# First attention of a two-layer kernel: TensorE's second pair of score maxima set directly behind the scores

## The reference, cut to what matters

```python
def _L0_xattn_ref(x, y, wq, bq, wk, bk, wv, bv, wo, bo):   # 16 heads of 8
    q = (x @ wq + bq).reshape(B, Sq, H, D).transpose(0, 2, 1, 3)
    k = (y @ wk + bk).reshape(B, -1, H, D).transpose(0, 2, 1, 3)
    v = (y @ wv + bv).reshape(B, -1, H, D).transpose(0, 2, 1, 3)
    scores = jnp.einsum('bhqd,bhkd->bhqk', q, k) / jnp.sqrt(jnp.asarray(D, x.dtype))
    attn = jax.nn.softmax(scores, axis=-1)
    out = jnp.einsum('bhqk,bhkd->bhqd', attn, v)
    return out.transpose(0, 2, 1, 3).reshape(B, Sq, E) @ wo + bo
...
x = x + _L0_xattn_ref(_layernorm(x, axis=-1), ctx_768, ...)
x = x + _L0_ffn_ref(_layernorm(x, axis=-1), ...)
x = x + _L1_xattn_ref(_layernorm(x, axis=-1), ctx_768, ...)
x = x + _L1_ffn_ref(_layernorm(x, axis=-1), ...)
```

## Time and profile before

| what | value |
|---|---|
| median of 3 runs | 514.8 us |
| lowest and highest run | 514.21 and 516.99 us |
| span of the profiled execution (first to last instruction) | 513.1 us |
| TensorE busy | 487.3 us (95% of the span) |
| VectorE, ScalarE, GpSimd busy | 354.2, 288.2, 234.4 us |
| first attention, rounds 2 to 13 | from about 32 to 95 us in the trace |

### The profile page before, as it was taken

How to read it: one execution, slowest core, us unless ns; L and a number is a source line. 1 busy time by engine, 2 the same in 40 slices (tenths; PEclk the granted TensorE clock), 3 DMA queues, 4 the chain that set the end, 5 groups by cost and what they waited for, 6 DMA issues and landing times.

```text
span 513.1 us, 13570 instructions
## 1 busy us (share of the span) xinstructions
PE 487.3 (95%) x5109; PEld 378.7 (74%) x5113; DVE 354.2 (69%) x1000; ACT 288.2 (56%) x984; POOL 234.4 (46%) x331
## 2 busy tenths in 40 slices
PE   4799999998999999999999999899999999999996
PEld 3466766656668778887787777788757897799995
DVE  5888989766786678566786665757866588535553
ACT  3366566463586776666867657665664444413332
POOL 4845545035365544575444755324231980090440
PEclk9699999999999999999999999999999999999999
DMA  8900000000001100111000000022202100000001
GB/s 229 234 3 4 3 3 3 3 1 8 4 1 32 34 20 16 34 33 34 3 2 2 4 3 3 1 66 64 64 0 71 56 0 1 1 22 24 1 2 42
DMA packets 21872, 14.48 MB, mean 28 GB/s; under 512 B 5928, under 2 KB 21136, under 8 KB 21808
## 3 DMA queue, kind: packets, MB, share of 16 engines
q1 hardware_dynamic: 20704, 13.31, 9.6%
q10 hardware_dynamic: 1104, 0.30, 0.3%
HBM read 12.30 MB, written 1.05 MB: 26 GB/s over the span
## 4 chain that ended last, share of the span: by engine, by line
PE 79%; DVE 12%; ACT 3%; issue 2%; DMA 1%; POOL 1%; ACTq 0%; DVEq 0%; POOLq 0%
PE bank L1792 9%; PE bank L1721 6%; PE bank L1551 5%; PE bank L1558 5%; PE bank L1801 5%; PE bank L1538 5%; PE bank L1510 5%; PE bank L1374 5%; PE bank L1463 5%; PE bank L1521 4%; PE bank L1530 4%; PE bank L1808 3%; PE bank L1609 3%; PE bank L1359 3%; ACT work L1150 2%
## 5 line engine op out<-in xcount | busy, mean ns | idle before, releaser
L1150 ACT ACTIVATE work<-bank,negmax 128x124 f32<-128x124 f32 x256 | 90.0, 387 | 52.2 <-DVE ipa_s L775 52.0
L498 POOL TENSOR_TENSOR work<-work,rsum 128x496 f32<-128x496 f32 x64 | 64.1, 1012 | 120.2 <-DVE rsum L789 120.2
L533 POOL TENSOR_SCALAR work<-work,slot 128x128 f32<-128x128 f32 x64 | 49.7, 792 | 48.3 <-DVE slot L864 29.4
L1150 ACT ACTIVATION_READ_ACCUMULATOR work<-bank,negmax 128x1 f32 x256 | 58.9, 230 | 0.0
L1792 PE MATMUL bank<-work 128*128 128x256 f32 x224 | 53.4, 381 | 0.0
L1014 DVE SCALAR_TENSOR_TENSOR work<-work,bank 128x256 f32<-128x256 f32 x64 | 26.9, 421 | 33.0 <-ACT work L1302 32.8
L1302 ACT ACTIVATE work<-bank 128x256 f32<-128x256 f32 x64 | 24.5, 383 | 40.6 <-PE bank L1792 29.1
L481 POOL TENSOR_TENSOR work<-work 128x512 f32<-128x512 f32 (+2 forms) x48 | 39.2, 817 | 12.1 <-DVE work L745 9.6
L306 DVE TENSOR_TENSOR x_all<-bank,x_all 128x128 f32<-128x128 f32 x16 | 4.7, 292 | 57.4 <-PE bank L1721 55.4
L1792 PEld LDWEIGHTS bank<-work 128*128 128x128 f32 x224 | 40.3, 190 | 4.7 <-DVE work L1017 0.2
L773 DVE TENSOR_REDUCE negmax<-bank 128x4 f32<-128x496 f32 x64 | 42.5, 664 | 0.0
(11 more groups left out here) (197 smaller groups left out, 1101.1 us busy)
## 6 DMA issues: line engine op xcount, KB each, us to landing
work<-in_L_ffn_w_dram SPq DMA_DIRECT2D x42, 128.0 KB, 2.3
x_all<-in_x_dram SPq DMA_DIRECT2D x4, 256.0 KB, 5.8
out_dram<-x_all SPq DMA_DIRECT2D x4, 256.0 KB, 2.6
ctx_all<-in_ctx_dram SPq DMA_DIRECT2D x4, 192.0 KB, 6.0
ctx_all<-in_L_ffn_w_dram SPq DMA_DIRECT2D x6, 128.0 KB, 2.3
work<-in_L_xattn_Wq_dram SPq DMA_DIRECT2D x1, 512.0 KB, 6.5
work<-in_L_xattn_Wo_dram SPq DMA_DIRECT2D x1, 512.0 KB, 8.2
work<-in_L_ffn_We_dram SPq DMA_DIRECT2D x1, 512.0 KB, 5.7
```

Source lines behind the costliest of these rows:

```text
L498: pool.tensor_tensor(part, part, rsum1[:, b % 2, CH * n:CH * n + CH].unsqueeze(2).broadcast_to((128, CH, ORG)), ALU.mult).then_inc(Z.norm, 1)
L533: ins = pool.tensor_scalar(ohw_of(e)[:, k, :], count[:, :], slot[:, h, 0, k, e % E1:e % E1 + 1], slot[:, h, 1, k, e % E1:e % E1 + 1], ALU. ...
L1150: ins = act.activation(p1[:, b % 2, n, c, 0:ORG], blocks(bank[n])[:, c, 0:ORG], ACT.Exp, bias=negmax1[:, b % 2, h:h + 1], accum_out=sums1[ ...
```

## The change

In TensorE's `round0(b)` for b of 2 and more, the second pair of maxima is issued directly behind the scores. Before, it stood behind the projection and the turned maxima. Rounds below 2 keep their order. No instruction is added or removed.

```diff
                     if there(b):
                         scores0(b)
+                    if there(m):
+                        maxima0(m, 1)
                     after(pe, A.o, min(y + 1, B))
                     if spare(b):
                         pe.wait_ge(A.xT, min(a + 1, B))
...
                         project0(y)
                     if there(n):
                         turn0(n)
-                if there(m):
+                if b < FILL and there(m):
                     maxima0(m, 1)
                 if there(t):
                     values0(t)
```

## The result

The changed kernel took 523.65 us (median of 6 runs, 522.45 to 525.08). The kernel before, run beside it, took 516.47 us over its now 6 runs (514.21 to 517.93). The ratio is **1.0141, 95% interval 1.0117 to 1.0164**: 7.2 us slower. The forecast was 6.9 us slower at 521.7 us, with a range up to 523.6; the measured median lies 0.05 above that end.

What follows compares the result with a forecast made beforehand. The start of the turned maxima was taken to set the round, through VectorE back to TensorE's transpose. Losses of 4.41 + 0.90 + 1.26 + 0.31 = 6.9 us on 514.8 gave 521.7 us, range 518.0 to 523.6.

Steps and rivals of the forecast that it cites:

- The wait ahead of pair 1: TensorE, behind the scores: pair 1 waits 0.31 us for VectorE's first reduction, loading 2.76 after the round's transpose (T).
- Pair 1 ahead of the projection: TensorE: pair 1, now first, holds the projection and the turned maxima back by a further 0.32 us.
- The period: Normal round, transpose to transpose: 5.22 becomes 5.85 us, closed from the turned maxima through VectorE to the normalized input.
- TensorE's own loop: The round through TensorE alone would close at 5.13 us before and 5.44 after, shorter than the period.
- By rounds: Loss by rounds: seven normal ones 4.41 us, rounds 6 and 10 0.90, 11 and 12 1.26, 13 0.31.
- the slow L597: VectorE's normalized input in rounds 6 and 10: took 0.56 us in place of 0.33, expected to be normal after the change.
- Nothing later wins it back: Behind round 13 the chain lies on TensorE with no transfer waited for, so the whole 6.9 us stays.
- A: Transpose does not wait for the normalized input; VectorE has slack, only TensorE's delay counts: 4.1 us slower, 518.9; chance 0.14.
- B: Slow input stays in rounds 6 and 10, projection takes 0.39 behind pair 1: 1.3 us more, 523.0; chance 0.08.
- C: TensorE saves a change between 32 and full rows, if the first reduction ends early: 512.9 us; 0.06, shared with no change.
- D: TensorE's added idle time lowers its granted clock in the stage: tens of us lost if half-clocked; chance 0.02.
- term for the level of the kernel before: Last step: the kernel before's median, 514.8 us, 1.7 above its profiled span of 513.1, to which 6.9 was added.

Runs made afterwards that it cites:

- e2: Changed kernel with VectorE's reduction of pair 0 cut to 32 of 128 columns, the rest left out; ratio to the kernel before 0.9988.
- e1: Kernel before, with pair 1 of the maxima moved between the projection and the turned maxima in rounds 2 to 13; ratio to the kernel before 1.0113.
- e4: Changed kernel with VectorE's normalized input put ahead of its second reduction in rounds 2 to 10; ratio to the kernel before 1.0102.
- e6: Kernel before, with VectorE's normalized input put ahead of its second reduction in rounds 2 to 10; ratio 0.9966, and 0.9972 when run again.
- e10: Kernel before, with pair 0's reduction cut to 32 of 128 columns and the normalized input ahead of the second reduction; ratio 0.9947.
- e9: Changed kernel with pair 0's reduction cut to 32 of 128 columns and the normalized input ahead of the second reduction; ratio to the kernel before 0.9948.

## Why the prediction was right in its mechanism and its range too short

Point by point, by its own steps:

- **The wait ahead of pair 1**: forecast 0.31 (T + 2.76), measured 0.32 (T + 2.77). Right. e2 shows that it is VectorE's reduction that is waited for: shortened, the wait is gone, whatever engine the row names; in round 10 the changed kernel's own row names it.
- **Pair 1 ahead of the projection**: forecast 0.32, measured 72.31 - 71.97 = 0.34. The nearest row was the right one for a TensorE that has been waiting. But the two terms are not separate costs: with the wait gone, pair 1 starts 0.15 sooner behind the scores than the projection did and delays the turned maxima by only 0.17 (e2), so taking the wait away saves 0.50 and not the 0.31 of its term.
- **The period**: forecast 5.85, measured 5.88. The turned maxima set it (e1), through VectorE's chain to the normalized input (e4, e6).
- **TensorE's own loop**: forecast 5.13 in the old order and 5.44 in the new one, measured 5.07 (e6, e10) and 5.44 (e4). The second is luck: the loop was taken 0.06 too long and its growth as 0.31, where it is 0.37. It did not set the period, so the sum was not touched.
- **By rounds**: seven normal rounds gave 0.66 each (4.6 against 4.41); rounds 6 and 10 gave 0.39 each (0.78 against 0.90), since the slow L597 vanished as supposed and less of the variances came through (the reciprocal starts 0.20 ahead of the transpose, 74.88 against 75.08, not 0.12); rounds 11 to 13 gave 16.95 - 15.20 = 1.75 (against 1.57). In all 7.2 against 6.9.
- **Nothing later wins it back**: right, stage and kernel lost the same.
- **Rivals**: A is out (its rounds would have been some 5.55 long, and the transpose names the normalized input). B is out: the slow input did not stay, and the projection came 0.34 behind pair 1, not 0.39; that its 523.0 us lie nearer to the measured median than the forecast is luck. C's mechanism exists, worth 0.14 a round (e9), but the condition that it needed was not met. D is out: clock 1.00.

**The step that failed** is the last one, from the sum to the median: its term for the level of the kernel before, "the median, 1.7 above it, 514.8". Six runs put that level at 516.47 us (514.21 to 517.93), 1.7 us higher. The 514.8 was the median of three runs, and the profiled span of 513.1 that the step leaned on belongs to an execution near the lowest of the six: in the changed kernel, time less span of the profiled execution is 525.08 - 523.4 = 1.7 us, so the one before took about 514.8. The terms of the sum were a little short as well, 7.2 measured against 6.9: rounds 11 to 13 gave 0.2 more than forecast and the seven normal rounds 0.2, rounds 6 and 10 gave 0.1 less. Of the 1.95 us between 521.7 and 523.65, 1.67 are the level and 0.28 the terms; with either alone the median would have stayed below 523.6 (523.4 and 522.0).

So the range was too short at its upper end. It left 0.6 us above rival B for the spread of the runs, less than the level was off, while round 2 alone starts at 32.67 and 33.92 us in two traces of the changed kernel. The 0.05 us by which the median lies outside are themselves within that spread: the second measurement of the changed kernel gave 523.47.

## What to carry to other kernels

Where an instruction waits for another engine in the middle of a full engine's order, look at what stands ahead of it: it may be the cover that hides the wait. Ask who waits for the steps that a moved one passes: here they were the start of the chain that closed the round, while VectorE could not take the moved step's result any earlier. A few runs' median carries its own uncertainty into a forecast in microseconds, so the range has to hold that as well as the terms. The round in which something else delays the awaited step is where an exposed wait shows first, as rounds 6 and 10 did in e9.

## What the runs showed of the hardware

- Weights were loaded well ahead of their matmul while other matmuls still ran on the same rows: in e2 pair 1's weights load at 69.53 and its matmul starts at 69.88, while the scores, on all four groups of 32 rows, run until 70.09 by their modelled ends. Behind a wait, load and matmul were 0.03 apart (71.97 and 72.00 in the changed kernel).
- The same two matmuls cost TensorE a different time by their neighbours: with both holds gone (e9 and e10), a round lasts 4.93 when they stand next to the scores, which use 32 rows as well, and 5.07 when they stand between full-array work and the values. Behind the first matmul of the scores pair 1 starts after 0.96 to 0.98 (e2, e9), the projection after 1.12 (before, e10).
- VectorE to TensorE took 0.11 to 0.13 from the end of the reduction to the load that waited for it (77.13 to 77.24 before, 71.84 to 71.97 in the changed kernel, 69.41 to 69.53 in e2).
